# Masks and row maxima by halves of two boards in the attention of layers 1 and 3

## The reference

```python
q, k, v = split_heads(h @ Wq), split_heads(h @ Wk), split_heads(h @ Wv)      # 4 heads of 64
sim = jnp.einsum('bhid,bhjd->bhij', q, k) * scale
sim = jnp.where(adjacency_mask[:, None, :, :], sim, neg)
attn = jax.nn.softmax(sim, axis=-1)
out = jnp.einsum('bhij,bhjd->bhid', attn, v)
return out.transpose(0, 2, 1, 3).reshape(...) @ Wo + bo
```

## Time and profile before

| | |
|---|---|
| median of 3 runs | 2009.05 us (2006.77 to 2009.29) |
| the profiled execution | 2007.06 us, its span 2005.1 us |
| TensorE busy (matmul) | 1840.9 us, 92% |
| VectorE busy | 1380.0 us, 69% |
| ScalarE busy | 996.7 us, 50% |
| mean granted TensorE clock | 0.967 of full speed |

### The profile page before, as it was taken

How to read it: one execution, slowest core, us unless ns; L and a number is a source line. 1 busy time by engine, 2 the same in 40 slices (tenths; PEclk the granted TensorE clock), 3 DMA queues, 4 the chain that set the end, 5 groups by cost and what they waited for, 6 DMA issues and landing times.

```text
span 2005.1 us, 58180 instructions
## 1 busy us (share of the span) xinstructions
PE 1840.9 (92%) x23611; PEld 1636.5 (82%) x23611; DVE 1380.0 (69%) x3777; ACT 996.7 (50%) x3707; POOL 153.3 (8%) x265
## 2 busy tenths in 40 slices
PE   6999999899999999999999999999998999999997
PEld 5878888878888878888878887878887888888886
DVE  4576677676777676777676677676767676677674
ACT  4455455454455454455455455455455445455452
POOL 0000000000000000000000000000000000000000
PEclk8899999999999999999999999899999999999898
DMA  6000000000000000000000000000000000000000
GB/s 195 1 9 13 13 8 12 13 8 13 13 8 13 12 8 13 13 8 12 13 13 8 13 13 8 12 13 8 13 13 8 12 13 8 13 13 8 12 7 6
DMA packets 36564, 30.62 MB, mean 15 GB/s; under 512 B 11600, under 2 KB 36176, under 8 KB 36368
## 3 DMA queue, kind: packets, MB, share of 16 engines
q1 hardware_dynamic: 36368, 27.48, 4.6%
HBM read 19.08 MB, written 8.39 MB: 14 GB/s over the span
## 4 chain that ended last, share of the span: by engine, by line
PE 75%; DVE 16%; issue 4%; ACT 4%; DMA 0%; DVEq 0%; SPq 0%; POOL 0%; POOLq 0%
PE ps L477 68%; PE ps L589 3%; PE ps L663 3%; DVE small L1069 2%; ACT probs L893 2%; DVE f L1228 1%; DVE xn L1081 1%; DVE f L1226 1%; DVE small L1075 1%; DVE oT L968 1%; DVE x L1233 1%; DVE kT L1128 1%; DVE probs L1158 1%; DVE probs L1142 1%; PE ps L786 1%
## 5 line engine op out<-in xcount | busy, mean ns | idle before, releaser
L477 PE MATMUL ps<-hT,w_hi 128*128 128x256 f32 x2560 | 487.8, 284 | 3.1 <-DVE w_lo L968 1.6
L477 PE MATMUL ps<-w_hi,hT 128*128 128x256 f32 (+1 forms) x1536 | 424.6, 344 | 0.0
L477 PEld LDWEIGHTS ps<-hT,w_hi 128*128 128x128 f32 x2560 | 406.6, 190 | 6.9 <-DVE w_lo L968 2.0
L893 ACT ACTIVATE probs<-probs,small 128x64 f32<-128x64 f32 x1024 | 342.0, 337 | 92.3 <-DVE small L1148 90.7
L477 PE MATMUL ps<-hT,w_lo 128*128 128x256 f32 x1280 | 332.8, 282 | 0.0
L477 PEld LDWEIGHTS ps<-w_hi,hT 128*128 128x128 f32 x1536 | 268.3, 188 | 42.7 <-DVE wh L1200 11.5
L464 POOL TENSOR_TENSOR small<-small,consts 128x1 f32<-128x1 f32 x256 | 151.3, 591 | 1824.6 <-DVE small L1077 1824.6
L477 PE MATMUL ps<-w_hi,oT 128*128 128x256 f32 x768 | 204.7, 331 | 57.6 <-DVE oT L968 48.4
L477 PE MATMUL ps<-w_lo,hT 128*128 128x256 f32 (+1 forms) x768 | 250.0, 337 | 0.0
L477 PEld LDWEIGHTS ps<-hT,w_lo 128*128 128x128 f32 x1280 | 243.5, 190 | 0.0
L477 PEld LDWEIGHTS ps<-w_hi,oT 128*128 128x128 f32 x768 | 147.9, 212 | 76.2 <-DVE oT L968 65.2
(11 more groups left out here) (126 smaller groups left out, 3329.8 us busy)
## 6 DMA issues: line engine op xcount, KB each, us to landing
x_next<-x SPq DMA_DIRECT2D x32, 256.0 KB, 2.7
out<-x SPq DMA_DIRECT2D x32, 256.0 KB, 2.2
raw_lo<-mats SPq DMA_DIRECT2D x6, 1024.0 KB, 10.5
adj<-adjq SPq DMA_DIRECT2D x64, 16.0 KB, 2.2
raw_hi<-mats SPq DMA_DIRECT2D x1, 1024.0 KB, 11.6
adjT<-adjt SPq DMA_DIRECT2D x64, 8.0 KB, 2.3
raw_lo<-mats SPq DMA_DIRECT2D x1, 512.0 KB, 8.3
raw_consts<-board_consts SPq DMA_DIRECT2D x1, 451.5 KB, 3.1
```

Source lines behind the costliest of these rows:

```text
L477: return nc.tensor.matmul(o, lhsT, rhs, start=start, stop=stop, skip_group_check=True)
L893: last = fn(p, p, ACT.Exp, bias=ROWMAX[s][:, row:row + 1], accum_out=ROWSUM[s][:, row:row + 1])
```

## The change

For layers 1 and 3 (a > 0) the steps "mask" and "max" of VectorE get a new content. The step "mask" of a unit now masks the columns 0 to 127 (boards 0 and 1) and takes their two row maxima; the step "max" masks the columns 128 to 255 (boards 2 and 3) and takes theirs. The second half of each signals the old semaphores `masked` and `rowmax`, the first half two new ones, `masked_h` and `rowmax_h`. ScalarE's exponentials of boards 0 and 1 wait for `rowmax_h`, those of boards 2 and 3 for `rowmax`. Layer 0 is as before, and ORDER is as before.

```diff
-        FOUR = ["e_ps", "wh_ps", "wh_sb", "ct_hi", "ct_lo"]
+        FOUR = ["masked_h", "rowmax_h", "e_ps", "wh_ps", "wh_sb", "ct_hi", "ct_lo"]
...
                     u, m, j, cj = i
-                    act.wait_ge(sm["rowmax"], v.eight[u])
                     for b in range(NB):
+                        if a > 0 and b == 0:
+                            act.wait_ge(sm["rowmax_h"], v.four[u - 4])
+                        elif b == (NB // 2 if a > 0 else 0):
+                            act.wait_ge(sm["rowmax"], v.eight[u])
                         at, row = (cj * NB + b) * SQ, m * NB + b
...
+                elif k in ("mask", "max") and a > 0:
+                    u, m, j, cj = i
+                    half = ("mask", "max").index(k)
+                    b0, cols = half * NB // 2, slice(half * P, half * P + P)
+                    if half == 0:
+                        dve.wait_ge(sm["s_ps"], v.eight[u])
+                    p = rows(PR[s][:, j, cj * TOK + half * P:cj * TOK + half * P + P])
+                    stt(p, rows(bank(s, m)[:, cols]), scale, rows(MASKA[s][:, cols]), ALU.mult, ALU.add
+                        ).then_inc(sm[("masked_h", "masked")[half]], 1)
+                    dve.wait_ge(sm[("masked_h", "masked")[half]], (v.four[u - 4], v.eight[u])[half])
+                    nc.vector.reduce_max(ROWMAX[s][:, m * NB + b0:m * NB + b0 + NB // 2], p, AX_X, negate=True
+                                         ).then_inc(sm[("rowmax_h", "rowmax")[half]], 1)
```

## The result

The changed kernel takes 2120.3 us (median of 6 runs, 2112.66 to 2133.87) against 2007.78 us: a ratio of 1.058, 95% interval 1.0543 to 1.0616. Slower was forecast, but by 21 us, not 113. The profiled execution took 2124.97 us, its span is 2123.0 us and the mean granted clock of TensorE 0.926 instead of 0.967.

The account below looks back on a forecast made before the run. The prediction took TensorE, standing still for VectorE at places A and B, as the bound. 2007.1 us plus 18.0 (12.9 at A, 4.5 at B, 0.6 at the ends) plus 3 for clock gave 2028.1, forecast 2029, range 2014 to 2042.

Parts of the forecast that it names:

- The price of a half: On VectorE, a mask or maximum of 128 columns would take 0.28 us, where 256 columns take 416 to 418 ns.
- the steps of 0.32 and 0.20: On VectorE, start-to-start time behind a 128-column operation: 0.32 us for a dependent successor, 0.20 us for an independent one.
- +0.23 at A in layer 1: Place A, slot 0's layer 1: later probabilities delay TensorE 0.23 us (bounds 0 and 0.30), 15 times.
- +0.63 at A in layer 3: Place A, slot 1's layer 3: the second half of `oT`, awaited by TensorE, comes 0.63 us later, 15 times.
- `oT` at B: Place B, slot 0's layer 3: reciprocal, `oT` and waiting TensorE 0.28 us later, 16 times, 4.5 us.
- the exponentials without a taker: Places A and B: exponentials starting 0.27 us earlier gain nothing, since the probabilities wait for VectorE.
- Nothing is saved on TensorE, SP or GpSimd, no DMA moves: Whole kernel: the change saves no time on these engines and moves no DMA; 0 us in the sum.
- I take 3 us, from -5 to +12: TensorE's clock: a quarter more falls, 4 steps (1.7 us lost full clock, 1.2 us longer each), 4.6 us, partly hidden.
- Partly hidden: Rival, chance 0.15: only layer 3's 0.63 us at the 15 places A remains, 9.5 us; 2015 to 2019 us.
- no difference: Rival, chance 0.07: shifts as worked, but a dozen clock falls are lost, repaying 14 us; 2011 us.
- faster: Rival, chance 0.06: same mechanism at A and B, but 19 clock steps go; 4 us less, 2003 us.
- Dearer: Rival, chance 0.10: a half costs 352 ns, 2050 us; or 0.28 us with a dozen more clock steps, 2039 us.

Follow-up runs that it names:

- e5: Kernel before with VectorE's loop written out and the halved masks and maxima in layer 1 alone: 2010.85 us, ratio 1.003.
- e6: Kernel before with VectorE's loop written out and the halved masks and maxima in layer 3 alone: 2045.67 us, ratio 1.0199.
- e2: Changed kernel with 80 semaphore increments that nobody waits for ahead of VectorE's loop: 2055.9 us, ratio 1.0251.
- e9: Changed kernel, VectorE's loop written out, all four exponentials of a unit waiting for both halves' maxima: 2047.48 us, ratio 1.02.
- e1: Kernel before with 32 semaphore increments that nobody waits for ahead of VectorE's loop, the loop unchanged: 2076.98 us, ratio 1.0358.
- e3: Changed kernel with VectorE's loop written out, its 16 iterations following each other: 2044.43 us, ratio 1.0211.
- e4: Kernel before, no halves, with VectorE's loop written out, as a control: 1999.89 us, ratio 0.997.
- e8: Kernel before, no halves, VectorE's loop written out, one added addition (0.60 us) ahead of layer 3's bias addition: 2033.47 us, ratio 1.0119.

## Why the prediction was wrong

**The direction and the local mechanism were right.** The price of a half (0.28 us, measured 282 and 286 ns), the steps of 0.32 and 0.20, +0.23 at A in layer 1 (e5: 0.21), +0.63 at A in layer 3 (e6: 0.61), the sum of both at A of 0.86 (e2: 0.88), `oT` at B, and the exponentials without a taker (e9) came out as worked. The lengths of the masks and maxima sum to 38.7 us more (145.6 instead of 106.9), as the forecast's 38; the page's busy time rose by 29 only, since it counts the time in which two operations overlap once. The Trainium skill (VectorE: DVE Perf Modes, "The DRAIN you can't avoid") has a rule that an operation starts only once the pipeline is empty, and in the same section lets an operation that is not held start earlier, which the prediction left out. The estimate from the rule alone would have been too high; VectorE starts an operation 0.20 us behind the start of a 0.28 us one (969.28 to 969.48).

**The step that failed:** "Nothing is saved on TensorE, SP or GpSimd, no DMA moves". The sum took VectorE's added instructions as time on VectorE only. They are also code ahead of a loop and in it, and for that the sum has no term. The loop starts 12 instructions later and is 16 longer, and with that its return stands on "issue" and the instruction queue moves 5 more packets each time: its first instructions are no longer at hand. e1 shows this alone to be worth 72 us (3.58% of 2006), after against e3 74 us (1.058 less 1.0211). Of it 37 us are the idles themselves, 14 by 2.65. Most of the rest goes with the clock: e1 loses 108 us of full clock instead of 66, which is 25 steps of 1.7 us, and at the prediction's 1.2 us for each some 30 us, an estimate. Some of these falls can be placed. Behind 13 of the 14 returns of the changed kernel and 11 of the 14 of e1 the clock falls 22 to 30 us after the first mask of place B, where it falls in no run without slow returns. The loads from 1048.69 on in the changed kernel are such a case, in layer 0, where TensorE's loads follow each other without a break. Whether what is left, some 5 us, is work pushed into each other was not tested.

The Trainium skill (Runtime: NRT & Kernel Launch, "Instruction fetch mechanics") says that most engines, TensorE not among them, keep 512 instructions in two blocks of 256, and that a taken branch to a block no longer held stalls for a fetch. The traces agree as to the stall. With these figures the five layouts (instructions ahead of the loop and in it: 251 and 308 kept, 282 and 308 not, 330 and 308 kept, 263 and 324 not, 342 and 324 kept) fit together, as an estimate from that page, if the loop of the kernel before starts 177 to 204 instructions into a block. That offset was chosen to fit and the block size was not measured, so the runs show that place decides, not why. The counts 308 and 324 could have been read before the run, but the runs alone told on which side of the border they lie.

**The term that was mis-sized:** the clock, "I take 3 us, from -5 to +12". Without the fetches the halves cost 48 us over e4, of which 18 are the shifts, so some 30 us go with the clock: e3 loses 108 us of full clock, e4 60. The price of a step was about right (28 steps at 1.2 us are 34 us); their number was not, 28 instead of 4. I had taken the falls as proportional to TensorE's idle time at A and left B out. They grow faster than the idle time. From A to B TensorE's idle time at full clock rose by a fifth (length less busy, 3.85 us in e4 and 4.57 in e2), while the steps within 22 us of the first mask rose at A from 18 in e4 (16 in the earlier trace rows's kernel) to 32 in e3, and at B from 9 to 24. A wait of 0.6 us at a place where the clock already falls in part of the iterations is paid about three times here, once as itself and twice as clock. That a wait without halved operations does this is shown by e8, for about two thirds of what layer 3's halves cost.

Of the rivals none described the loss. "Partly hidden", "no difference" and "faster" were each refuted by e5, e6 and e2. "Dearer" in its form with a dozen more clock steps, 2039 us, was nearest to e3's 2044, still with too few steps.

## What to carry to other kernels

Count instructions, not only their time: on VectorE a loop body of some 300 instructions stood near a border here, and code ahead of the loop counted too. The sign is an engine idle on "issue" at the first instruction of the loop, as many times as it returns, and more packets on the instruction queue. What takes the cost away is a move of the loop's start or writing the loop out. The move must be the right one: 32 increments ahead of the loop brought the cost in, 80 took it away, and these 80 had VectorE's first operation start at 15.5 us instead of 8.4.

Before splitting an operation to release its reader earlier, look whether the reader's own reader is there to take the result; here it was VectorE itself, made later by the split. And where TensorE's clock already falls in part of the iterations, price a new wait at more than its length; here it was about three times.

## What the runs showed of the hardware

- A slow return of VectorE's loop cost 2.5 to 2.9 us of idle time and 5 packets on q14 (70 more for 14 returns), with an unchanged loop (e1).
- Some 4400 to 4600 instructions of VectorE in order showed no idle for fetching: e3 has none on "issue", and e4 runs at 0.997 of the kernel with a loop.
- Executions of one kernel differ by their clock: e4's ten runs go from 1992.84 us at a clock of 0.974 to 2015.48 us at 0.960. That spread is as large as many changes.
- A delay of 0.60 us on VectorE at two places of an iteration (e8) lowered the mean granted clock from 0.970 to 0.950 (profiled executions; medians 0.9695 and 0.952).
